# Attention of a vision tower: the plan takes its float32 K from DRAM instead of from the sum of two float16 halves

## The reference, cut to what matters

```python
qn = q / (jnp.linalg.norm(q, axis=-1, keepdims=True) + 1e-08)
C = 1.0 - jnp.einsum('bhnd,bhmd->bhnm', qn, qn)
C = jnp.where(eye, DIAG_VAL, C)
log_K = -C / OT_REG
for _ in range(SINKHORN_ITERS):          # 10
    log_u = log_marg - logsumexp(log_K + log_v[..., None, :], axis=-1)
    log_v = log_marg - logsumexp(log_K + log_u[..., :, None], axis=-2)
z = jnp.exp(log_u[..., :, None] + log_K + log_v[..., None, :])
z = z / jnp.max(z, axis=(-2, -1), keepdims=True)
z = jnp.where(eye, 1.0, z)
attn = jax.nn.softmax(z * scale, axis=-1)
out = jnp.einsum('bhnm,bhmd->bhnd', attn, v)
```

## Time and profile before

| | |
|---|---|
| median of 3 runs | 4995.21 us (4989.33 to 4996.69) |
| the profiled execution, its own time | 4997.56 us |
| its span, first to last instruction | 4995.8 us |
| share of the span: TensorE, VectorE, ScalarE | 92%, 74%, 62% busy |
| share of the 16 DMA engines, all queues | 16.7% |

### The profile page before, as it was taken

One profiled execution on the slowest core, in us unless ns is written; L12 is line 12 of the kernel. 1 busy time (PEld: TensorE's weight loads), 2 busy tenths in 40 slices (PEclk: granted clock), 3 DMA queues, 4 the chain that ended last, 5 costly groups with the idle time before them and its releaser, 6 DMA issues. The chain is left out here.

```text
span 4995.8 us, 192120 instructions
## 1 busy us (share of the span) xinstructions
PE 4573.8 (92%) x84693; PEld 3640.3 (73%) x84710; DVE 3718.4 (74%) x8486; ACT 3097.0 (62%) x4620; POOL 313.9 (6%) x347
## 2 busy tenths in 40 slices
PE   5999999975899999999999999999999879599992
PEld 3777777732688888888888888888888745277771
DVE  8999999944478888887887887777777745355556
ACT  4777777723566666666666666666666326377776
POOL 0000000000000000000000000000000005523331
PEclk9999999987899999999999999999999979699996
DMA  1010000023001111111111122100000024322224
GB/s 64 28 40 28 27 27 27 17 93 81 25 17 32 29 37 29 33 25 23 42 43 36 37 42 52 27 23 16 16 16 15 6 89 158 126 65 72 68 69 162
DMA packets 190201, 232.97 MB, mean 47 GB/s; under 512 B 81024, under 2 KB 159104, under 8 KB 187328
## 3 DMA queue, kind: packets, MB, share of 16 engines
q1 hardware_dynamic: 175872, 189.76, 14.0%
q0 software_dynamic: 13632, 32.66, 1.8%
HBM read 144.09 MB, written 78.25 MB: 45 GB/s over the span
## 5 line engine op out<-in xcount | busy, mean ns | idle before, releaser
L699 PE MATMUL y_ps<-k_sb,x_sb 128*12 128x256 f16 x58368 | 1694.9, 274 | 33.5 <-DVE x_sb L956 24.3
L699 PEld LDWEIGHTS y_ps<-k_sb,x_sb 128*12 128x12 bf16 x58368 | 1427.8, 88 | 218.2 <-issue 37.6
L829 ACT ACTIVATE y_sb<-y_ps 128x256 f32<-128x256 f32 x912 | 348.4, 382 | 856.2 <-PE y_ps L699 856.2
L838 ACT ACTIVATE k_new<-cos,k_bias 128x512 f32<-128x512 f32 x768 | 520.9, 683 | 171.7 <-PE cos L726 171.7
L709 PEld LDWEIGHTS turned_x<-rows_in,y_sb 128*128 128x128 f32 x3648 | 478.3, 191 | 120.2 <-issue 72.7
L987 DVE CUSTOM_DVE_ANT_0 plan<-plan,u_rows,v_last 128x512 f32<-128x512 f32 x768 | 535.2, 744 | 4.1
L709 PE MATMUL turned_x<-rows_in,y_sb 128*128 128x16 f32 x3648 | 527.1, 258 | 9.9 <-ACT y_sb L829 9.2
L257 PE MATMUL acc<-w_hl,feat_h 128*128 128x384 f16 x2688 | 455.3, 327 | 87.5 <-ACT feat_h L242 87.5
L852 ACT ACTIVATE plan<-plan,p_bias,p_scale 128x1024 f32<-128x1024 f32 x384 | 464.1, 1237 | 9.7 <-DVE p_scale L998 9.7
L975 DVE TENSOR_TENSOR plan<-k_sb 128x1024 f32<-128x1024 f16 x384 | 459.3, 1217 | 0.0
L1002 DVE TENSOR_TENSOR k_sb<-k_new,k_sb 128x2048 f16<-128x2048 f32 x192 | 436.2, 2272 | 29.8 <-ACT k_sb L846 29.8
(11 more groups left out here) (261 smaller groups left out, 7223.1 us busy)
## 6 DMA issues: line engine op xcount, KB each, us to landing
x_in_sb<-expert_rows SPq DMA_DIRECT2D x39, 528.0 KB
xt<-in_x_dram SPq DMA_DIRECT2D x16, 1280.0 KB, 5.8
q_left<-q_parts SPq DMA_DIRECT2D x192, 64.0 KB, 3.9
q_right<-q_parts SPq DMA_DIRECT2D x192, 64.0 KB, 3.9
raw<-in_w_dram SPq DMA_DIRECT2D x24, 384.0 KB, 4.3
w<-w_halves SPq DMA_DIRECT2D x16, 576.0 KB, 7.1
w<-expert_results SPq DMA_DIRECT2D x24, 384.0 KB, 6.4
v_parts<-v_sb SPq DMA_DIRECT2D x16, 408.0 KB, 2.4
```

What stands on the lines that cost most here:

```text
L699: last = nc.tensor.matmul(y[a][32 * c:32 * c + XW, :, :], high[:, j, XW * h:XW * (h + 1)], k_sb[s][:, h, :, at:at + P], start=(h == 0 and ...
L829: nc.scalar.activation(y_sb[a][:, :, :], y[a][:, :, :], ACT.Copy).then_inc(rows_read[a], 1)
L838: nc.scalar.activation(k_new[h % 2][:, c, :], cos[:, c % 2, :], ACT.Exp, bias=k_bias[:, 0:1], scale=1.0 / (REG * Q_SCALE ** 2), accum_out= ...
```

## The change: K is stored to DRAM when it is made and loaded again when the plan needs it

In the build part, each head's float32 K (`k_new`, 128 partitions of 2048 elements, 1024 KB) is also stored by SP to a ring in DRAM with five places of four heads. In the fin part, SP loads it from there into `plan[h]`, of which there are now four instead of two. The join on VectorE is gone, and `times_u` waits for the load instead. `exponents` now also waits until the store of the head before last has landed, since it overwrites the same buffer. `high_parts` loses its wait for the join. SP's list of a phase gets four stores and four loads of 1024 KB, each with its own wait, in an order that is written out in the diff. The semaphores of the stage before are handed to `attend` and cleared by SP at its start. The plan's K is now the float32 value itself rather than the sum of its halves.

```diff
--- before.py
+++ after.py
@@ -477,6 +477,8 @@
                 nc.vector.tensor_copy(q_hl[a][:, 1, :, :], pq_t[:, 1, :, :]).then_inc(parts_read, 1)
 
             images(dve, nothing, split, read_low)
+    return counters
+
 
 GH = 4
 GROUPS_PER_IMAGE = HEADS // GH
@@ -490,6 +492,7 @@
 PIECE_OF = [(part, k) for part, pieces in ((0, EXPERTS), (1, EXPERTS), (2, EXPERTS * DIM // P)) for k in range(pieces)]
 PIECES = len(PIECE_OF)
 LARGEST_FROM, MAX_PHASE, SPLIT_FROM = 3, 18, 20
+RING = 5
 K_SHIFT = float(15 * np.log(2))
 HIDE = -60000.0
 ATT_SCALE = HD ** -0.5
@@ -501,7 +504,7 @@
         eng.wait_ge(counter, START + count)
 
 
-def attend(nc, q_parts, v_parts, ident, pick_rows, att, w, w_halves, unscale):
+def attend(nc, q_parts, v_parts, k_all, ident, pick_rows, att, w, w_halves, unscale, over):
 
 
 
...
@@ -569,8 +572,8 @@
             [sem(f"turned3{a}") for a in range(2)], [sem(f"x_steps{a}") for a in range(2)], [sem(f"x_new{a}") for a in range(2)])
         first_steps, first_x, x_turned, xt_ready = sem("first_steps"), sem("first_x"), sem("x_turned3"), sem("xt_ready3")
         cos_ready, k_exp, k_high, k_built = sem("cos_ready"), sem("k_exp"), sem("k_high"), sem("k_built")
-        joined, u_rows_ready, plan_ready, head_max_ready = (
-            sem("joined"), sem("u_rows_ready"), sem("plan_ready"), sem("head_max_ready"))
+        u_rows_ready, plan_ready, head_max_ready = sem("u_rows_ready"), sem("plan_ready"), sem("head_max_ready")
+        k_out, k_in = [sem(f"k_out{a}") for a in range(2)], [sem(f"k_in{h}") for h in range(GH)]
         max_rows_ready, all_max_ready, scale_ready, p_ready = (
             sem("max_rows_ready"), sem("all_max_ready"), sem("scale_ready"), sem("p_ready"))
         pv_ready, pv_read, pv_turned, den_ready, att_ready = (
@@ -623,6 +626,16 @@
             def store(image, s):
                 dst = att[bass.ds(image, 1), :, :, :].rearrange("a p b (s n) -> (a p) b s n", s=3)[:, :, s, :]
                 sp.dma_start(dst, att_sb[s][:, :, :, :].rearrange("p b h d -> p b (h d)")).then_inc(att_out[s], 16)
+
+            def store_k(G, h):
+                H = (G + 1) * GH + h
+                after(sp, k_exp, (H + 1) * TB)
+                sp.dma_start(k_all[(G + 1) % RING, h, :, :], k_new[h % 2][:, :, :].rearrange("p b n -> p (b n)")).then_inc(k_out[h % 2], 16)
+
+            def load_k(F, h):
+                after(sp, pv_ready, (F - 1) * GH + h + 1)
+                after(sp, k_out[h % 2], 16 * ((F * GH + h) // 2 + 1))
+                sp.dma_start(plan[h][:, :, :].rearrange("p b n -> p (b n)"), k_all[F % RING, h, :, :]).then_inc(k_in[h], 16)
 
             def load_raw(n, times):
                 part, k = PIECE_OF[n]
@@ -665,16 +678,28 @@
                 if old:
                     after(sp, pv_turned, (G - 3) * GH)
                     load_v(t - 1 if s == 0 else t, (s + 2) % 3)
+                if build:
+                    store_k(G, 0)
+                if fin:
+                    load_k(G - 2, 3)
                 if tail:
                     after(sp, att_ready, (G - 2) * GH)
                     store(t - 1, s)
-
+                for h in range(1, GH):
+                    if build:
+                        store_k(G, h)
+                    if old:
+                        load_k(G - 1, h - 1)
+
+            for counter in over:
+                sp.sem_clear(counter)
             sp.wait_ge(zeroed, START + ZEROS)
             phases(sp, phase)
             for s in range(3):
                 sp.wait_ge(att_out[s], START + 16 * IMAGES)
             for a in range(2):
                 sp.wait_ge(parts_out[a], START + 16 * PIECES)
+                sp.wait_ge(k_out[a], START + 16 * ALL_GROUPS * GH // 2)
 
         @block.tensor
         def _(pe):
...
@@ -833,22 +858,21 @@
                 for c in chunks:
                     if c == 0:
                         after(act, k_built, H - 1)
+                        after(act, k_out[h % 2], 16 * (H // 2))
                     if c % 2 == 0:
                         after(act, cos_ready, H * 2 + (c // 2 + 1))
                     nc.scalar.activation(k_new[h % 2][:, c, :], cos[:, c % 2, :], ACT.Exp, bias=k_bias[:, 0:1],
                                          scale=1.0 / (REG * Q_SCALE ** 2), accum_out=row_sums[s][:, c, h:h + 1]).then_inc(k_exp, 1)
 
-            def high_parts(G, s, h, fin):
+            def high_parts(G, s, h):
                 H = (G + 1) * GH + h
                 after(act, k_exp, (H + 1) * TB)
-                if fin:
-                    after(act, joined, (G - 2) * GH + h + 1)
                 nc.scalar.activation(k_sb[s][:, h, 0, :], k_new[h % 2][:, :, :].rearrange("p b n -> p (b n)"), ACT.Copy).then_inc(k_high, 1)
 
             def weights(F, h, half):
                 if half == 0:
                     after(act, scale_ready, F * GH + h + 1)
-                part = plan[h % 2][:, 2 * half:2 * half + 2, :]
+                part = plan[h][:, 2 * half:2 * half + 2, :]
                 nc.scalar.activation(part, part, ACT.Exp, bias=p_bias[:, 0:1], scale=p_scale[h % 2][:, 0:1]).then_inc(p_ready, 1)
 
             def high_of(n):
@@ -893,7 +917,7 @@
                             weights(G - 2, b - 2, 1)
                     if c == 1 and build:
                         exponents(G, new, a, (2, 3))
-                        high_parts(G, new, a, fin)
+                        high_parts(G, new, a)
                     if c == 2 and build:
                         exponents(G, new, b, (0, 1))
                     if c == 2 and 0 <= 2 * (G - SPLIT_FROM) + f < PIECES:
@@ -905,7 +929,7 @@
                             exponents(G, new, b, (2,))
                     if c == 4:
                         if build:
-                            high_parts(G, new, b, fin)
+                            high_parts(G, new, b)
                         if fin:
                             read_v(G - 2, a)
 
@@ -967,24 +991,14 @@
                 else:
                     split(tr[1], s, x_steps[1], (G - 1) * (OLD - 1) + i, x_new[1])
 
-            def join(F, s, h, half):
-                H = F * GH + h
-                if half == 0:
-                    after(dve, pv_ready, H - 1)
-                cols = slice(half * 2 * TOKENS, (half + 1) * 2 * TOKENS)
-                done = nc.vector.tensor_tensor(plan[h % 2][:, 2 * half:2 * half + 2, :].rearrange("p b n -> p (b n)"),
-                                               k_sb[s][:, h, 0, cols], k_sb[s][:, h, 1, cols], ALU.add)
-                if half == 1:
-                    done.then_inc(joined, 1)
-
             def times_u(F, s, h, chunks):
                 H = F * GH + h
                 if chunks[0] == 0:
-                    after(dve, joined, H + 1)
+                    after(dve, k_in[h], 16 * (F + 1))
                     after(dve, u_rows_ready, H + 1)
                     nc.vector.memset(idle[:, :], 0.0)
                 for c in chunks:
-                    last = nc.vector.tensor_tensor_reduce(plan[h % 2][:, c, :], plan[h % 2][:, c, :], u_rows[:, :],
+                    last = nc.vector.tensor_tensor_reduce(plan[h][:, c, :], plan[h][:, c, :], u_rows[:, :],
                                                           v_last[s][:, c, h:h + 1], 0.0, ALU.mult, ALU.max, row_max[:, c:c + 1])
                 if c == TB - 1:
                     last.then_inc(plan_ready, 1)
@@ -1063,17 +1077,12 @@
                         if f == 1 and fin:
                             normalise(G - 2, new, a - 2, t_fin)
                         if fin:
-                            join(G - 2, new, a, 0)
-                            join(G - 2, new, a, 1)
                             times_u(G - 2, new, a, (0, 1))
                     if c == 1 and fin:
                         times_u(G - 2, new, a, (2, 3))
-                        join(G - 2, new, b, 0)
                     if c == 2:
                         if build:
                             low_parts(G, new, a)
-                        if fin:
-                            join(G - 2, new, b, 1)
                     if c == 3:
                         if f == 0 and tail:
                             normalise(G - 3, mine, GH - 1, t - 1)
@@ -1966,14 +1975,15 @@
     h = scratch("h_tokens", (IMAGES, P, TB, DIM), F32)
     q_parts = scratch("q_parts", (IMAGES, 2, DIM, TOKENS), F16)
     v_parts = scratch("v_parts", (IMAGES, P, TB * HEADS * VW), F32)
+    k_all = scratch("k_all", (RING, GH, P, TB * TOKENS), F32)
     att = scratch("att_tokens", (IMAGES, P, TB, DIM), F32)
     halves = scratch("w1_halves", (P, EXPERTS, 3, FFN), F16), scratch("w2_halves", (P, EXPERTS * FB, 2, DIM), F16)
     with ExitStack() as ctx:
         soft_rows_out, soft_results_out = soft_semaphores(nc, ctx, "rows_out"), soft_semaphores(nc, ctx, "results_out")
         clear(nc, embed(nc, x, freqs, w_tok, h))
-        project(nc, h, wqv, ident, q_parts, v_parts)
+        over = project(nc, h, wqv, ident, q_parts, v_parts)
```

(6 more changed lines are left out.)

## The result

The changed kernel takes 5169.83 us (median of 4 runs, 5158.37 to 5176.51) against 4992.27 us before (4984.15 to 4996.69), a ratio of 1.0356 with the interval 1.0338 to 1.0375. It is slower by 178 us. I had forecast 5024 us, slower by 29, with a range up to 5085. The direction and the kind of the loss were as forecast; the price was five to six times too small, and the range did not hold it.

The account below looks back on a forecast made before the run. TensorE was taken as the bound, 55.65 us a phase, not VectorE. Joins 0, run-out -6 and late instruction pages +35 made +29 us: 5026.6 from the profiled 4997.56, 5024 as median; range 4985 to 5085.

Parts of the forecast that it names:

- That the joins set nothing: Phases 2 to 46: removing 384 joins, 459.3 us of VectorE, gains 0, or 10.9 us if the chain was read wrong.
- The argument from the quiet phases: Phases 35 to 45, without work on experts' weights: TensorE busy all 612.20 us, so 55.65 us is a phase's floor.
- the 0.37 us wait: TensorE's repeated wait for VectorE in weight phases, cycle 9: its chain starts on ScalarE without a join, so 10.9 us stay.
- The run-out: Phases 48 and 49 at the end: joins gone between normalisation and `times_u`, -6 us, bounds -4.7 and -9.6.
- Stores and loads in time: The 192 stores and 192 loads land after some 5.1 us, costing 0 while a transfer lands in under 15 us.
- rival C: Phases 20 to 33: a transfer lands late and `exponents` holds ScalarE and both chains; about 5090 us, chance 0.07.
- Late pages: TensorE's 16 KB instruction pieces, fetched by DMA, delayed by the added transfers: +35 us, bounds 0 and 163.
- two rates: TensorE time lost per us of DMA time added: 0.062 from phases 5 to 17, 0.145 from phases 21 to 34.
- The signs for a quiet phase: Phases 35 to 45: 0.5 to 1.5 us over 55.65, TensorE waiting for "issue", DMA share near 0.45.
- my own upper bound: Cost of delayed instruction fetches if all 1125 us of added DMA time cost 0.145 each: 163 us.
- half of the transfers are free because they stand alone: Only transfers right behind another were counted, 563 us of DMA time; a single one holds an engine 2.9 us, under 4.7.
- The slow clock: After an "issue" stop TensorE runs part of the time at 1.2 instead of 2.4 GHz; included in the loss per DMA us.

Follow-up runs that it names:

- The last but one version: Kernel before with each phase's weight transfers in two parts and the next young group's first vector made ahead of the last cycle's weight work: 0.9951.
- the paced pieces: Changed kernel with each 1024 KB transfer as four of 256 KB, stores as chunks are made, loads spread over ten cycles: 1.0081 times the kernel before.
- the last version of the kernel before: Kernel before with weight transfers in two parts, first vector made earlier, and q loads in four pairs over cycles 2, 3, 7, 8: 0.9928, 4962.58 us.

## Why the prediction was wrong in size and right in kind

*That the joins set nothing.* Right. The argument from the quiet phases (TensorE busy for all 612.20 us) holds: without joins and without transfers the gain is 0.12% (0.9970 to 1.0006). The chain ahead of the 0.37 us wait has no join in it, as read: the changed kernel has it 29 times for 12.2 us, like the one before. That VectorE sets nothing at all would be too much. The last but one version removes that wait by making the vector ahead of the weight work (0.94 us at L1009 in the earlier trace rows), so that VectorE's order did set it.

*The run-out.* Right. Forecast -6 us. From the last mark (the end of phase 47) to the end of the span it is 1051.6 us before and 1045.7 after. This alone would prove little, as the five kernels with joins on the three chips that agree scatter from 1043.9 to 1051.6. Phase 49 by itself is clear: up to its last `times_v` matmul it takes 39.2 us in all the kernels with joins and 33.8 to 34.1 in all those without. In it `times_u` now starts right behind the normalisation, where the earlier trace rows has 2.35 us of joins:

```profile
4169.58 0.22 DVE L1053 TENSOR_TENSOR att_sb<-pv,den 128x64 f32<-128x64 f32 x1
4169.73 0.75 DVE L1001 CUSTOM_DVE_ANT_0 plan<-plan,u_rows,v_last 128x512 f32<-128x512 f32 x1
```

*Stores and loads in time.* Right, rival C did not come: neither ScalarE ahead of L864 (`exponents`) nor VectorE ahead of `times_u` waits for a DMA. The landing of 5.1 us that I worked out was 4.8 for a store and 6.9 for a load, far from the 15 that would hurt:

```profile
k_all<-k_new SPq DMA_DIRECT2D x192, 1024.0 KB, 4.8
plan<-k_all SPq DMA_DIRECT2D x192, 1024.0 KB, 6.9
```

*Late pages.* This is the step that failed, in size. The term was +35 us and measured +188 (phases 2 to 47). I had two rates, 0.062 and 0.145 us lost for each us of DMA time, took the lower one, and then counted only half of the transfers because "a single one holds an engine 2.9 us, less than the 4.7 us that a page lasts". Both choices were wrong. The signs for a quiet phase were 0.5 to 1.5 us more at a DMA share near 0.45; it took 3.9 us more at 0.52. The quiet phases gained (0.52 x 59.56) - 3.9 = 27.1 us of DMA time and lost 3.9 us each, which is 0.144, the higher rate. Over phases 2 to 47 it is 188.1 us for 0.52 x 2776.7 - 0.14 x 2588.6 = 1081 us of DMA time, 0.174, so that even the higher rate was too low. Taken over all transfers the higher rate gave 163 us, my own upper bound, and I let the range end at half of it. What I overlooked is what the higher rate stood for: phases 21 to 34 were those in which several large transfers and the q loads were in the queue together, and this is what four stores and four loads a phase make of every phase. The lower rate was that of phases with a shorter queue. The rows did tell that the loss per us more than doubled from one stretch to the other; a cost that grows so is not to be carried on at its lower slope when the DMA share goes from 0.14 to 0.52.

That half of the transfers are free because they stand alone was an assumption without a row. The 192 stores alone, none of them next to a load of K, cost 20 us (31 in the trace), the 192 loads alone 75 (64). Taking stores and loads 3 to 8 us apart left the loss at 4.1%.

*The slow clock.* It was in the rates, and it is part of the difference. In phases 2 to 47 the trace's record of the granted clock has TensorE at 1.2 in place of 2.4 GHz for 6.8 us before and for 75.1 after, so that 34 us of full-clock time more are missing. This is over half of the 59.4 us of busy time that the same matmuls took more. The other 25 us are, as I estimate, the ends of the matmuls ahead of the stops: a record of `multiply` lasts 0.27 us, but 64 of them together take 1.92 us, 0.03 each, so that each stop has some 0.24 us of it counted as busy, and 101 more waits for "issue" (112 against 11) make 24 us. With the idle time that accounts for the 188.

*What stays open.* That TensorE stops because its own instructions are late is shown by the pages that land ahead of 82 of 84 stops (before, ahead of 6 of 7). That bunched transfers make them late, and the same bytes spread out far less so (17 pages over 3 us late in place of 67), is shown by the paced pieces at a DMA share of 0.58, and by the last version of the kernel before. How a page waits is not settled. Smaller packets do not shorten the wait, and a page gets no better chance between two transfers of 512 KB. The Trainium skill has each DMA engine go round robin between the queue rows it has work for (DMA: Bandwidth & Descriptors, "Queues, rings and completion order"), by which a page should wait for one turn of SP's queue and not for all of it. The runs cannot see a turn; what they show is that halving the transfers changed nothing (1.0343 twice), and that packets of a quarter of the size did not shorten the wait, as I had expected of short turns. Nor can I say why stores alone cost 0.4% and loads alone 1.5%, or why both cost 3.5%. The late pages show the same growth (1, 15, 21 and 67 of them), but not what makes it. A page that is a little late after one transfer and meets the next one before it has caught up would do it, but that was not tried by itself.

## What to carry to other kernels

If TensorE is at its floor and its program is long and unrolled, look at the DMA queue as a shared resource of its instruction stream: "issue" waits of one or two microseconds, each behind a burst of transfers and ending soon after a page of the instruction queue has landed, are the sign. What hurt here was how much stood in the queue at once far more than how much was moved; issue transfers in pieces and spread them over the time that is there, before moving more bytes. And where a trace gives two rates for a cost, and the higher one belongs to the stretch with more traffic, a change that adds far more traffic goes by the higher one.

## What the runs showed that I had not expected

In the quiet phases the same 8.4 MB of K a phase cost TensorE 0.1 us in 256 KB pieces spread over the phase, at a DMA share of 0.58, and 3.9 us in 1024 KB transfers, at a share of 0.52. (The version with the weight transfers in two parts as well has 0.3 us there.) Two transfers of 512 KB in a row are as bad as one of 1024 KB. And the price is not additive: 0.4% for the stores, 1.5% for the loads, 3.5% for both. TensorE goes on about 1.4 us after the page has landed that it waited for (the median of the 84 stops).
